# Loading a group's keys as six transfers of 16 partitions instead of three broadcasts, in a cross-attention kernel

## The reference

```
q = x @ W_q;  k, v = text @ W_k, text @ W_v;  k_ip, v_ip = ip @ W_k_ip, ip @ W_v_ip     (split into heads)
probs  = softmax(q k^T * 16**-0.5)                      # 512 x 508 for each batch and head
qsem   = l2norm(probs @ text)                           # 512 x 512 for each batch and head
fused  = q k_ip^T * 16**-0.5 + 0.5 * qsem @ l2norm(ip)^T
out    = probs @ v + (softmax(fused) * mask) @ v_ip     # mask: one value per query row
result = out @ W_out + b_out + x
```

## Time and profile before

| | us |
|---|---|
| median of 3 runs | 1828.28 (1827.54 to 1833.78) |
| the profiled execution | 1832.93 |
| its span, first to last instruction | 1831.2 |
| TensorE matmul busy in the span | 1742.6 |
| VectorE, ScalarE, GpSimd busy | 1244.5, 1184.2, 1231.0 |

### The profile page before, as it was taken

How to read it: one execution, slowest core, us unless ns; L and a number is a source line. 1 busy time by engine, 2 the same in 40 slices (tenths; PEclk the granted TensorE clock), 3 DMA queues, 4 the chain that set the end, 5 groups by cost and what they waited for, 6 DMA issues and landing times.

```text
span 1831.2 us, 48590 instructions
## 1 busy us (share of the span) xinstructions
PE 1742.6 (95%) x14421; PEld 1106.2 (60%) x14421; DVE 1244.5 (68%) x2872; ACT 1184.2 (65%) x2644; POOL 1231.0 (67%) x1414
## 2 busy tenths in 40 slices
PE   4999999499999999999999999999999999999899
PEld 2767766356666566666566666656566666666455
DVE  5445454267777677777677777767677777777684
ACT  3444555367777677777677777767677777777321
POOL 3122112278888788888788888878788888888310
PEclk8899999799999999999999999999999999999999
DMA  5354553736777777765665686666657656854133
GB/s 160 109 144 134 137 171 106 142 72 91 91 100 112 89 93 100 113 91 91 104 91 89 101 117 92 101 93 102 86 85 115 91 89 100 99 90 77 38 101 100
DMA packets 427592, 187.95 MB, mean 103 GB/s; under 512 B 384728, under 2 KB 415072, under 8 KB 427392
## 3 DMA queue, kind: packets, MB, share of 16 engines
q1 hardware_dynamic: 425088, 183.40, 59.0%
q10 hardware_dynamic: 2304, 2.14, 0.4%
HBM read 67.21 MB, written 34.39 MB: 55 GB/s over the span
## 4 chain that ended last, share of the span: by engine, by line
POOL 39%; PE 27%; issue 24%; DMA 3%; DVE 3%; POOLq 2%; ACT 1%; SPq 1%; ACTq 0%; DVEq 0%
POOL probs L587 17%; POOL probs L594 17%; PE bank L1287 13%; PE bank L1495 3%; PE bank L1430 3%; POOL reduced L602 2%; POOL wkv L580 2%; PE bank L1431 2%; DMA late<-wkv 2%; PE bank L1345 2%; PE bank L1496 1%; POOL reduced L601 1%; PE bank L1395 1%; PE bank L1404 1%; DVE reduced L1018 1%
## 5 line engine op out<-in xcount | busy, mean ns | idle before, releaser
L1430 PE MATMUL bank<-u_sb,late 127*128 127x508 f16 x2560 | 946.2, 376 | 0.0
L1431 PE MATMUL bank<-u_sb,late 127*128 127x508 f16 (+3 forms) x2560 | 763.0, 298 | 0.0
L1091 DVE TENSOR_REDUCE neg_max<-bank 128x1 f32<-128x508 f32 x640 | 439.1, 686 | 368.5 <-PE bank L1395 368.4
L580 POOL TENSOR_TENSOR wkv<-probs,wkv 128x508 f16<-128x508 f32 x320 | 358.6, 1121 | 219.6 <-ACT wkv L817 219.4
L1429 PE MATMUL bank<-v_ring,late 127*128 127x41 f16 x2560 | 468.8, 183 | 12.5 <-DMA late<-wkv 8.0
L1100 DVE SCALAR_TENSOR_TENSOR probs<-bank,probs 128x508 f32<-128x508 f32 x640 | 432.5, 676 | 6.3 <-PE bank L1431 6.3
L1429 PEld LDWEIGHTS bank<-v_ring,late 127*128 127x128 f16 x2560 | 247.2, 97 | 245.6 <-DMA late<-wkv 10.7
L594 POOL TENSOR_TENSOR probs<-probs,late 128x508 f32<-128x508 f32 x320 | 368.6, 1152 | 0.0
L587 POOL TENSOR_TENSOR probs<-probs,wkv 128x508 f32<-128x508 f32 x320 | 357.6, 1118 | 0.0
L1430 PEld LDWEIGHTS bank<-u_sb,late 127*128 127x128 f16 x2560 | 248.3, 97 | 167.5 <-issue 2.4
L1395 PE MATMUL bank<-x_sb,work 96*128 96x508 bf16 x640 | 242.1, 379 | 41.7 <-DMA x_sb<-k_parts 18.5
(11 more groups left out here) (166 smaller groups left out, 1804.7 us busy)
## 6 DMA issues: line engine op xcount, KB each, us to landing
x_sb<-in_x SPq DMA_DIRECT2D x16, 640.0 KB, 5.1
reduced<-in_ctx SPq DMA_DIRECT2D x32, 256.0 KB, 5.0
work<-q_parts SPq DMA_DIRECT2D x32, 240.0 KB
x_sb<-k_parts SPq DMA_DIRECT2D x32, 238.1 KB
u_parts<-u_sb SPq DMA_DIRECT2D x8, 825.5 KB, 4.2
u_sb<-u_parts SPq DMA_DIRECT2D x8, 825.5 KB, 5.3
v_parts<-v_sb SPq DMA_DIRECT2D x8, 820.0 KB, 8.2
v_ring<-v_parts SPq DMA_DIRECT2D x32, 205.0 KB, 9.0
```

Source lines behind the costliest of these rows:

```text
L580: nc.gpsimd.tensor_tensor(rows[:, 1, :, 0:TP], probs[:, j % PROB_RING, :].rearrange("p (k t) -> p k t", k=TT), rows[:, 0, :, 0:TP], ALU.su ...
L1091: nc.vector.tensor_reduce(neg_max[:, j % 4:j % 4 + 1], bank[S_BANK + j % 2][:, 0:T], AX.X, ALU.max, negate=True)\
L1430: nc.tensor.matmul(y, hi_k, u_sb[0:TP, par, GH[k]:GH[k] + T], start=(k == 0), stop=False)
L1431: done = nc.tensor.matmul(y[:, k * TP:T], hi_k, u_sb[0:TP, par, UL[k]:UL[k] + U_COLS[k]], start=False, stop=(k == TT - 1))
```

## The change

The keys of a group are loaded by six DMAs, each from the 16 DRAM rows of one part to 16 partitions, where there were three whose source repeats 16 rows three, two or one times. The waiting count follows: nine DMAs instead of six add to the semaphore. The queries' loads stay.

```diff
@@ load_group
                 eng.dma_start(q_ring[a0 * D:(a0 + copies) * D, n], q_parts[b, 0:copies, :, heads, :].rearrange("a d h s -> (a d) h s"))\
                    .then_inc(group_loaded[n], 16)
             for part, (a0, copies) in enumerate(((0, 3), (3, 2), (5, 1))):
-                eng.dma_start(k_ring[a0 * D:(a0 + copies) * D, n],
-                              k_parts[b, part, :, heads, :].unsqueeze(0).broadcast_to([copies, D, GROUP, T]))\
-                   .then_inc(group_loaded[n], 16)
+                for a in range(a0, a0 + copies):
+                    eng.dma_start(k_ring[a * D:(a + 1) * D, n], k_parts[b, part, :, heads, :]).then_inc(group_loaded[n], 16)
@@ scores
                 if j % (GROUP * ST) == 0:
-                    pe.wait_ge(group_loaded[n], 16 * 6 * (rnd + 1))
+                    pe.wait_ge(group_loaded[n], 16 * 9 * (rnd + 1))
```

## The result

The changed kernel takes 1803.76 us (median of four runs, 1799.01 to 1805.73) against 1827.91 us before: 0.9857, with a 95% interval of 0.9828 to 0.9885. The profiled execution has a span of 1803.2 us against 1831.2.

The account below looks back on a forecast made before the run. The prediction took TensorE as the bound, so the gain is what TensorE loses to transfers: 11.1 us at the start plus 7.5 in the stream, 18.6 us, giving about 1810 us, with 1804 to 1819 for 8 in 10.

Parts of the forecast that it names:

- (a): SyncE's issuing of group loads: six key issues cost 0.4 to 0.7 us more per load, 0 on TensorE's path.
- (b): First group's keys: TensorE's first score at 348.5 us, 6.8 us earlier, bounds 4.9 and 7.1.
- (c): First score to unit 0: `u_sb` just hidden, unit 0 starts 11.1 us earlier, bounds 6 and 12.
- (d): Stream of units, 30 loads: TensorE's waits for transposed tiles go, 7.5 us gained, bounds 0 and 8.0.
- Nothing that a load touches is late behind it: Stream of units: with even loads, nothing touched by a group's load comes late behind it; no separate size.
- `u_sb` not hidden: Start bound by bytes, unit 0 at 364 to 365 us; gain 14.5 us, time 1814 us; chance 0.20.
- start only: Transposed tiles in the stream stay late; gain 11.1 and perhaps 1 us, time 1816 us; chance 0.15.
- no other engines: Key loads: a 16-row load lands no sooner; gain 0 to 2 us, time 1827 us; chance 0.04.
- slower: Start and stream: key pieces pass one after another and delay tiles on all engines; 1860 us; chance 0.03.

Follow-up runs that it names:

- after_again: The changed kernel run once more, unchanged, for a second trace; ratio 0.9884 to the kernel before.
- rows_outside: Kernel before, still three key transfers per group, but the source's 16 rows as outer dimension and copies inside, queries' loads turned likewise; ratio 0.9838.
- one_broadcast: Kernel before with the threefold key broadcast kept and the twofold one replaced by two single copies; ratio 0.9898.

## Why the prediction was right and where it was wrong

The means of the six traces of either kernel split the difference of their spans, 1827.3 - 1802.3 = 25.0 us: query issue to unit 0, 30.4 - 19.2 = 11.2; tile waits as listed, 9.1; the rest of the stream, 1314.1 - 1312.0 = 2.2; loop-end stalls, 8.2 - 6.8 = 1.4; half of the time at half clock, 8.1 - 6.1 = 2.0; and the phases ahead of the loads and behind the stream 0.9 against.

(a) *SyncE's issue time, nothing on the path: right.* 2.73 us for six against my 2.8. Transposes are not quite always at 1.23 us: six of 320 took 2.0 to 3.5 us to issue, where I had said none over 2, and none of these made TensorE wait.

(b) *The first group: right.* Forecast 348.5 us, measured 349.10 and, in after_again, 348.44. The landing of the sixth copy, which I had bounded by 3.0 and 5.3 and taken as 3.3 us, took 3.7 us; 3.5 is the median of all key loads.

(c) *Unit 0 at 360.5 us, 11.1 us earlier: right, in part by luck.* It was 360.99. `u_sb` was hidden, with the thin cover that I gave it: the second load, issued at 351.5, landed at most 8.3 us later, by 359.8. But the even rate of 259 GB/s that I had put under this date did not come. The two stretches of the changed kernel in which first the groups and then mostly `u_sb` pass are:

```profile
342.00:355.00 13.00, 2.21 (x5) 0.35 (x5) 2.56 (x4) 4.40 (x7) 0.79 (x2) 0.50 1.05 197
355.00:358.00 3.00, 2.13 (x7) 1.28 (x7) 1.47 (x3) 2.65 (x7) 1.41 (x2) 0.50 1.01 410
```

The 197 GB/s are below the 210 at which I had `u_sb` late, and the 410 made up for it. None of the earlier trace rows has such a rate, nor the 1 to 2 us that I added for the semaphore.

(d) *The stream, 7.5 us: this is the step that failed.* The mechanism was right, the waits are gone to the last, and rows_outside and one_broadcast show the cause. The size was wrong, in two ways that the traces show. First, I took the sum from one execution, 8.0 us, and even set 8.0 as its upper bound; in eight traces with all the broadcasts in the stream it is 7.2 to 13.7 us, 9.7 on average. Second, a wait costs more than the idle time that is listed for it. TensorE's timeline of the kernel before around the wait that ended at 562.32 starts so:

```profile
560.50 0.37 PE L1395 MATMUL bank<-x_sb,work 96*128 96x508 bf16 x1
560.72 0.60 PE L1404 MATMUL bank<-ident,probs 128*127 128x128 f32 x4
```

and the same place in the changed kernel, with no wait, is:

```profile
540.26 0.37 PE L1394 MATMUL bank<-x_sb,work 96*128 96x508 bf16 x1
540.47 0.60 PE L1403 MATMUL bank<-ident,probs 128*127 128x128 f32 x4
540.91 0.18 PE L1428 MATMUL bank<-v_ring,late 127*128 127x41 f16 x1
```

From the score's start to the values' matmul it is 1.82 us with the wait and 0.65 without, so the wait cost 1.17 us where 0.99 are listed. The difference, 0.16 us before rounding, is the same at every such wait of this trace. My reading of it: matmul records overlap when nothing waits, and the weight load, else hidden under the matmul before, stands in the open. The list of waits of all engines has a row for it (kernel before, 372 to 1700 us) that I left out of account:

```profile
PEld bank L1429 <- DMA late<-wkv: 10.7, 14, 1.9
```

Summed over the trace of the kernel before, these excesses are 10.4 us instead of the listed 8.0 (11.4 on average over six traces instead of 9.1). That is the 2.2 us in the rest of the stream. The term was 11.3 us (9.1 + 2.2), not 7.5: of the 5.5 us between the forecast gain and that of the medians 3.8 are this.

What is left, 3.4 us on average over the traces, is loop-end stalls and half clock. *"Nothing that a load touches is late behind it"* holds so far as it goes. I had no term for what varies between executions, and took 4 us for its spread where executions of one and the same kernel in the later comparisons lie some 25 us apart (1820 to 1845). A range whose lower end was 12 + 8.0 us and these 4 us had no room for it: the sum with the right term, 11.1 + 11.3 = 22.4 us off 1827.91, is 1805.5, and 1803.76 is an ordinary draw around that. That the time fell just outside the range and not just inside is chance; that it lay well below 1810 is not.

The rivals: *`u_sb` not hidden* and *start only* are refuted by the wait lists above, *no other engines* by the landings. In *slower* the pieces would pass one behind the other; six of them, issued over 2.73 us, were landed 6.0 us after the first issue began (345.25 + 3.7 - 342.94), not 18. The Trainium skill gives a fixed cost of about 2 us for a DMA ("DMA: Bandwidth & Descriptors", "Anatomy of one DMA"), measured on transfers that GpSimd issues; these are SyncE's. Whatever it is here, it did not add up over the six. That page's section "Rules for kernel authors" also has the rule that decided this case: an outer dimension of size c below 16, such as a leading broadcast of c copies, confines a DMA to at most c engines. The DMA share of 0.18 and 0.13 and rows_outside agree with it. The coalescing rule of the same section, which I had weighed against the change, speaks of transfers under 64 KB. Pieces of 79.4 KB are over that, and here they cost TensorE nothing that a trace shows: rows_outside, with three transfers, had its first score later after the first query issue (8.2 us against 7.5).

## What to carry to other kernels

Look for stretches of a few us in which the DMA share is a small multiple of 1/16 at low GB/s: a transfer there may run on few engines, as the broadcasts did here, and what is queued behind it pays. In this kernel putting the 16 rows outside and the copies inside cured it as well as splitting the transfer did. When the gain is a sum of many short waits, take the weight loads' wait as well as the matmuls', and take more than one trace or a bound well above the one sum that you have.

## What was unexpected

- A DMA's issue can take long: behind a broadcast a transpose took up to 6.85 us to issue, and 66 to 74 of 320 took over 2 us in the kernels with all the broadcasts in the stream (43 in one_broadcast), one to six in the changed one.
- Issuing the first keys from a second engine gained nothing (first score at 351.11 us against 350.16).
- The stalls at loop ends (2 to 4 in an execution, 2.3 to 3.5 us each) change between executions of one kernel, and with them the half clock that follows them (6.8 to 21.9 us within a stream in all). The stream of the kernel before lay between 1332.6 and 1347.2 us by this and by the tile waits. Why a stall comes at a loop end in one execution and not in the next, and why 19 of the 58 were followed by no half clock, was not settled.
- The phase ahead of the loads varies too: in the changed kernel the first query issue came between 335.9 and 341.9 us.
